# Scores of a graph attention layer summed in column groups, and x strips 6 and 7 loaded by SyncE alone

## What is computed

```
h    = relu(layernorm(x))                       # x: 8192 x 256
hp   = inlayer2 @ W.T + b ; f1 = hp @ w1 + b1 ; f2 = hp @ w2 + b2
coef = softmax(leaky_relu(f1[:,None] + f2[None,:], 0.01) masked by adj > 0)   # 8192 x 8192
out  = x + coef @ h
```

## Time and profile before

| | |
|---|---|
| time, median of 3 | 1441.95 us |
| profiled execution | 1442.37 us, its span 1440.5 us |
| granted TensorE clock, mean | 0.992 |
| TensorE matmul busy | 1409.4 us (98%) |
| VectorE busy | 1280.3 us (89%) |
| ScalarE, GpSimd busy | 612.8 us (43%), 263.6 us (18%) |
| DMA | 302.43 MB, mean 210 GB/s |

### The profile page before, as it was taken

The page is one execution under the profiler, slowest core; times in us unless marked ns, Lnnn a source line. Parts: engine busy times, 40 slices in busy tenths (PEclk is TensorE's granted clock), DMA queues, the critical chain, the costliest instruction groups (busy, mean ns, idle before and its releaser), DMA issues.

```text
span 1440.5 us, 33339 instructions
## 1 busy us (share of the span) xinstructions
PE 1409.4 (98%) x12623; PEld 1245.9 (86%) x12623; DVE 1280.3 (89%) x1315; ACT 612.8 (43%) x713; POOL 263.6 (18%) x266
## 2 busy tenths in 40 slices
PE   8589999999999999999999999999999999999998
PEld 7378888888888888888888888888888888888887
DVE  5999999899898998989889898998989989899894
ACT  2895434444343443434444344443434434344330
POOL 0682111111110110111111011111101101111110
PEclk9799999999999999999999999999999999999999
DMA  9979999999999999999999999999999999999940
GB/s 292 321 174 210 231 232 231 232 233 216 209 210 207 218 209 209 215 206 213 211 212 210 207 216 209 210 216 208 210 207 217 210 208 216 207 212 213 210 106 13
DMA packets 110184, 302.43 MB, mean 210 GB/s; under 512 B 11732, under 2 KB 44628, under 8 KB 110164
## 3 DMA queue, kind: packets, MB, share of 16 engines
q1 hardware_dynamic: 100080, 289.52, 89.8%
q10 hardware_dynamic: 10084, 12.65, 3.0%
HBM read 293.73 MB, written 8.39 MB: 210 GB/s over the span
## 4 chain that ended last, share of the span: by engine, by line
PE 93%; DMA 2%; ACT 2%; SPq 1%; DVE 1%; issue 0%; ACTq 0%; DVEq 0%
PE acc L1048 61%; PE acc L1050 31%; DMA adj_sb<-in_adj_dram 1%; SPq L336 1%; DMA adj_sb<-in_L_gnn_inlayer_dram 1%; ACT h_f L582 1%; PE rp L1003 0%; ACT rp L566 0%; DVE wgt L837 0%; DVE wT L847 0%; PE rp L1011 0%; ACT mask L566 0%; DVE wT L731 0%; ACT H L588 0%; ACTq L336 0%
## 5 line engine op out<-in xcount | busy, mean ns | idle before, releaser
L1048 PE MATMUL acc<-H,wT 128*128 128x257 f16 x8192 | 1356.8, 274 | 8.0 <-DVE wT L847 4.5
L1050 PE MATMUL acc<-H,wT 128*128 128x257 f16 x4096 | 1120.3, 274 | 0.0
L1048 PEld LDWEIGHTS acc<-H,wT 128*128 128x128 bf16 x8192 | 802.3, 98 | 111.5 <-DVE wT L847 5.7
L566 ACT ACTIVATE mask<-adj_sb 128x1024 bf16<-128x1024 int32 x504 | 519.6, 1053 | 539.2 <-DVE wgt L837 430.9
L847 DVE STREAM_TRANSPOSE wT<-wgt 128x1024 f32<-128x1024 f32 x512 | 633.6, 1238 | 128.5 <-PE acc L1050 128.4
L837 DVE SCALAR_TENSOR_TENSOR wgt<-b_word,c_word,mask 128x1024 f32<-128x1024 f32 x504 | 627.8, 1258 | 0.0
L1050 PEld LDWEIGHTS acc<-H,wT 128*128 128x128 f16 x4096 | 401.5, 98 | 50.6
L486 POOL TENSOR_TENSOR x_res<-o_room,x_res 128x256 f32<-128x256 f32 x63 | 64.6, 1026 | 1099.6 <-ACT o_room L573 1072.7
L573 ACT ACTIVATE o_room<-acc,r_den 128x256 f32<-128x256 f32 x63 | 29.8, 473 | 234.4 <-DVE r_den L866 234.4
L491 POOL TENSOR_TENSOR o_room<-o_room,x_res 128x256 f32<-128x256 f32 x63 | 81.2, 1289 | 5.3
L488 POOL TENSOR_SCALAR o_room<-h_mean,no_nb 128x256 f32<-128x256 f32 x63 | 60.0, 953 | 0.0
(11 more groups left out here) (93 smaller groups left out, 163.7 us busy)
## 6 DMA issues: line engine op xcount, KB each, us to landing
adj_sb<-in_adj_dram SPq DMA_DIRECT2D x504, 512.0 KB, 8.6
x_res<-in_x_dram SPq DMA_DIRECT2D x64, 128.0 KB, 4.0
out_dram<-o_room SPq DMA_DIRECT2D x63, 128.0 KB, 4.3
H<-in_x_dram ACTq DMA_DIRECT2D x16, 256.0 KB, 12.9
H<-in_x_dram SPq DMA_DIRECT2D x16, 256.0 KB, 13.1
adj_sb<-in_adj_dram ACTq DMA_DIRECT2D x8, 512.0 KB, 14.8
wgt<-in_L_gnn_inlayer_dram ACTq DMA_DIRECT2D x8, 256.0 KB, 9.8
wgt<-in_L_gnn_inlayer_dram SPq DMA_DIRECT2D x8, 256.0 KB, 10.2
```

Source lines behind the costliest of these rows:

```text
L566: nc.scalar.activation(place, adj_sb[:, c, g * CQ:(g + 1) * CQ], ACT.Relu, scale=M_SCALE).then_inc(m_ready, 1)
L1048: pe.matmul(acc[:, par, 0:DV], w_hi[:, slot, t, :], H[:, j, part, 0:DV], start=(j == 0 and part == 0), stop=False)
L1050: mm = pe.matmul(acc[:, par, 0:DV], w_lo[:, slot, t, :], H[:, j, 0, 0:DV], start=False, stop=(j == ROWS - 1))
```

## The change

1. `f_of_strip` uses a `V` with a quarter of the columns and writes its 8 matmuls to four column groups of 32 output partitions; a new `f_sums` adds the four groups on TensorE, so `chunk_f` becomes `chunk_turn` (transpose) and, after `f_sums`, `chunk_max`. Chunk 0 is treated between `turn_in2(5)` and `turn_in2(7)`. After each strip but the last four 128x128 matmuls on `ones` are added (`keep_busy`).
2. ScalarE: `f_to_sbuf(1)` stands before `sums(1)`; `squares(1)` goes from before `D_big` to after c; VectorE's `raw_stats` 20 to 32 go behind `low` and in among the `pack`s.
3. x strips 6 and 7 come from the sync engine alone (it had half of each); of row 0's chunk 1 the scalar engine issues three quadrants, the sync engine one.
4. The masks of rows 0 and 1 get an order of their own (`mask_order`): row 0's (2,1) and (3,1) go ahead of row 1's (0,0) and (2,0). Row 1's second chunk is issued after (0,3,1), ahead of (1,2,0).
5. VectorE does `raw_stats(60, 64)` and `variance(7)` ahead of `weights(0,1,1)` and `low_of_values(7)` after it. GpSimd's `rstds(2)` and `rstds(7)` move.

```diff
@@ sync engine
-            load_x(sp, 4, 8, (0, 1))
-            first_adj(sp, 1, (0, 1))
+            load_x(sp, 4, 6, (0, 1))
+            load_x(sp, 6, 8, (0, 2, 1, 3))
+            first_adj(sp, 1, (0,))
@@ mask order, used by whoever waits for a mask
+        mask_order = ((0, 0, 0), (0, 1, 0), (0, 2, 0), (0, 3, 0), (0, 0, 1), (0, 1, 1), (0, 2, 1),
+                    (1, 0, 0), (1, 1, 0), (0, 3, 1), (1, 2, 0), (1, 3, 0), (1, 0, 1), (1, 1, 1),
+                    (1, 2, 1), (1, 3, 1))
@@ GpSimd
             rstds(0)
-            rstds(2)
             scale_D()
             affine(0)
+            rstds(2)
             rstds(1)
...
             D_column(4)
+            rstds(7)
+            affine(7)
             low_of_values(10)
-            rstds(7)
             D_column(5)
-            affine(7)
@@ ScalarE
             load_x(act, 4, 5, (2, 3))
-            sums(1)
             f_to_sbuf(1)
             load_x(act, 5, 6, (2, 3))
-            squares(1)
-            load_x(act, 6, 7, (2, 3))
+            sums(1)
             act.wait_ge(f2_rel_ready, 1)
...
-            load_x(act, 7, 8, (2, 3))
-            values(0)
             act.wait_ge(t_ps_ready, 1)
             nc.scalar.activation(c_f32...)
+            squares(1)
+            values(0)
             high_of_values(0)
             mask_part(0, 0, 0)
             mask_part(0, 1, 0)
-            first_adj(act, 1, (2, 3))
+            first_adj(act, 1, (2, 1, 3))
...
             mask_part(0, 1, 1)
+            mask_part(0, 2, 1)
             mask_part(1, 0, 0)
             mask_part(1, 1, 0)
+            mask_part(0, 3, 1)
+            second_adj(act, 1, (2, 3))
             mask_part(1, 2, 0)
             mask_part(1, 3, 0)
-            mask_part(0, 2, 1)
-            mask_part(0, 3, 1)
-            second_adj(act, 1, (2, 3))
@@ VectorE
-            for k in range(2, NS):
-                turn_in2(k)
-            chunk_f(0)
+            ... turn_in2(5)
+            chunk_turn(0)
+            turn_in2(6)
+            chunk_max(0)
+            turn_in2(7)
+            chunk_turn(1)
+            chunk_max(1)
             raw_stats(16, 20)
-            chunk_f(1)
-            raw_stats(20, 24)
...
+            raw_stats(24, 28)
             then_wait(pack_b(0))
+            raw_stats(28, 32)
             then_wait(pack_b(1))
+            variance(3)
...
             weights(0, 0, 1)
+            raw_stats(60, 64)
+            variance(7)
+            weights(0, 1, 1)
             low_of_values(7)
-            weights(0, 1, 1)
             weights(1, 0, 0)
@@ TensorE
+            def keep_busy(n):
+                for _ in range(n):
+                    pe.matmul(acc[:, 0, 0:P], ones[:, :], ones[:, :], start=True, stop=True)
             def f_of_strip(k):
                 pe.wait_ge(in2T_ready, 2 * (k + 1))
-                for m in range(FM):
-                    mm = pe.matmul(rp[:, k // SC, ...], V[:, m, :], in2T[:, k % 2, m, :], ...)
+                for e in range(2):
+                    for g in range(Q):
+                        m = 2 * g + e
+                        mm = pe.matmul(rp[B * g:B * (g + 1), k // SC, ...], V[:, m, :],
+                                       in2T[:, k % 2, m, :], start=(e == 0), stop=(e == 1))
+            def f_sums(c):
+                pe.wait_ge(f_cols_ready, c + 1)
+                for a in range(Q):
+                    mm = pe.matmul(f_sum_ps[B * a:B * (a + 1), c * ROWS:(c + 1) * ROWS], same[:, :],
+                                   parts[:, a, :, :, 0], start=True, stop=True)
+                mm.then_inc(f_sum_ps_ready, 1)
...
+            f_of_strip(7)
             pe.wait_ge(f2_of_ready, 1)
             b_exponents(0)
+            f_sums(1)
```

More of the change, by code:

```diff
@@ L139, in graph_attention @@
         F_ps = small[:, 1, 384:385]
+        f_sum_ps = small[:, 0, 256:256 + 2 * ROWS]
         hs_ps = small[:, 1, 0:D]
@@ L210, in graph_attention @@
         f_rows_ready = sem("f_rows_ready")
+        f_cols_ready = sem("f_cols_ready")
+        f_sum_ps_ready = sem("f_sum_ps_ready")
         f2_of_ready = sem("f2_of_ready")
@@ L291, in nth_part, with nth_mask @@
             return two_rows.index((I, g, c)) + 1 if first_two(I) else 8 * I + (Q * c + g + 1)
+        def nth_mask(I, g, c):
+            return mask_order.index((I, g, c)) + 1 if first_two(I) else 8 * I + (Q * c + g + 1)
         def nth_strip(I, k):
@@ L361, in second_adj @@
         def second_adj(eng, c, quadrants):
-            eng.wait_ge(m_ready, nth_part(0, Q - 1, c))
+            eng.wait_ge(m_ready, nth_mask(0, Q - 1, c))
             load_adj(eng, 1, c, quadrants)
@@ L667, in _ @@
             values(9)
+            high_of_values(9)
             values(10)
-            high_of_values(9)
             high_of_values(10)
@@ L755, in _, with chunk_turn, chunk_max @@
             dve.wait_ge(pick_ready, Q + 1)
[L756 to L761, removed]
+            nc.vector.tensor_copy(f2_of[:, :].rearrange("p (q s) -> p q s", q=Q),
+                                  same[:, :].rearrange("p (q v) -> p q v", q=Q)[:, :, Q].unsqueeze(2)
+                                  .broadcast_to([P, Q, B])).then_inc(f2_of_ready, 1)
+            def chunk_turn(c):
                 dve.wait_ge(f_rows_ready, c + 1)
                 dve.wait_ge(in2T_ready, 2 * SC)
-                then_wait(nc.vector.transpose(f_cols[:, c * CQ:(c + 1) * CQ], f_rows[:, c * CQ:(c + 1) * CQ]))
-                then_wait(nc.vector.tensor_copy(f_col[:, at, :], f_cols[:, c * CQ:(c + 1) * CQ].rearrange(
-                    "p (j o v) -> p j o v", o=2, v=B // 2)[:, :, :, 0]))
+                nc.vector.transpose(f_cols[:, c * CQ:(c + 1) * CQ], f_rows[:, c * CQ:(c + 1) * CQ]).then_inc(f_cols_ready, 1)
+            def chunk_max(c):
+                at = slice(c * ROWS // NCH, (c + 1) * ROWS // NCH)
+                dve.wait_ge(f_sum_ps_ready, c + 1)
+                then_wait(nc.vector.tensor_copy(f_col[:, at, :], f_sum_ps[:, c * ROWS:(c + 1) * ROWS].rearrange(
+                    "p (j o) -> p j o", o=2)))
                 then_wait(nc.vector.reduce_max(tiny[:, 6 + c:7 + c], f_col[:, at, 1], AX.X))
@@ L787, in variance @@
                                         ALU.add).then_inc(var_ready, 1)
-            for k in range(2, NS):
-                turn_in2(k)
-            chunk_f(0)
+            turn_in2(2)
+            turn_in2(3)
+            turn_in2(4)
+            turn_in2(5)
+            chunk_turn(0)
[4 more added lines that the diff above has]
+            chunk_max(1)
             raw_stats(16, 20)
-            chunk_f(1)
-            raw_stats(20, 24)
             dve.wait_ge(u_ready, Q + 1)
@@ L798, in _ @@
             nc.vector.reduce_max(tiny[0:1, 1:2], fm_ps, AX.X).then_inc(f_max_ready, 1)
-            variance(2)
-            raw_stats(24, 28)
             dve.wait_ge(F_ps_ready, 1)
@@ L809, in _ @@
             nc.vector.tensor_scalar(low[:, :], t_row[:, :], -1.0, 0.0, ALU.mult, ALU.min).then_inc(low_ready, 1)
-            variance(3)
+            raw_stats(20, 24)
+            variance(2)
             def low_of_values(n):
@@ L830, in weights @@
             def weights(I, g, c):
-                dve.wait_ge(m_ready, nth_part(I, g, c))
+                dve.wait_ge(m_ready, nth_mask(I, g, c))
                 if first_two(I) and c == 1 and g == 0:
@@ L905, in _ @@
             turn(1, 2)
-            raw_stats(60, 64)
             low_of_values(9)
             turn(0, 4)
-            variance(7)
             turn(1, 3)
@@ L921, in _ @@
             turn(0, 7)
+            low_of_values(15)
             turn(1, 6)
-            low_of_values(15)
             weights(2, 0, 0)
@@ L1018, in _ @@
             pe.wait_ge(u_ready, Q)
-            for k in range(NS):
-                f_of_strip(k)
+            f_of_strip(0)
+            keep_busy(4)
+            f_of_strip(1)
+            keep_busy(4)
+            f_of_strip(2)
+            keep_busy(4)
+            f_of_strip(3)
+            keep_busy(4)
+            f_of_strip(4)
+            keep_busy(4)
+            f_of_strip(5)
+            keep_busy(4)
+            f_sums(0)
+            f_of_strip(6)
+            keep_busy(4)
+            f_of_strip(7)
             pe.wait_ge(f2_of_ready, 1)
             b_exponents(0)
+            f_sums(1)
             pe.wait_ge(ident_ready, 1)
```

15 lines of the change are left out of this document (7 added, 8 removed).

## The result

The changed kernel takes 1449.26 us (median of 5, 1448.32 to 1452.15) against 1441.98 us for the kernel before on the same chip (5 runs, 1441.65 to 1442.88). The ratio is 1.0052, interval [1.0041, 1.0062]: slower by 7.3 us, where 4.9 were forecast. The profiled execution took 1448.32 us, its span 1446.4 us (before 1440.5: +5.9), its mean granted clock was 0.987.

What follows compares the result with a forecast made beforehand. Time was taken as the moment TensorE goes into unbroken work plus a constant: `turn(1,0)` +6.1 us, less the 1.20 us wait behind it, gives +4.9, 1446.8 us on the median; range 1439.8 to 1450.5.

Steps and rivals of the forecast that it cites:

- The forecast case: Load queues: x strips 6 and 7 starve beside adjacency, `turn(1,0)` slips; net +4.9 us, range 1444.7 to 1450, chance 0.50.
- the 3 us of the scores are eaten by the 4.1 us of squares that now stand behind them: ScalarE ahead of the first mask: the scores' lead is lost; -0.1 or +1.2 us at `weights(0,0,0)`, +0.5 taken.
- the two cases for `b_exponents(1)`: TensorE from 44.9 us: 1.88 us at full clock or 3.14 at half, so c ready at 48.7 or 50.0.
- `keep_busy` costs nothing: TensorE between the score strips: the added matmuls take no time, as TensorE waits for loads there.
- say moving at 57.0: Scalar queue: adjacency of row 0's chunk 1 starts moving at 57.0 us, leaving q1 alone from 55.4 for 0.4 MB.
- strip 6 is there at 66 us: Sign of being wrong: x strip 6 landed by 66 us, where 71.5 was forecast (bounds 67.5 and 73.5).
- `turn(1,0)` at 94.5: VectorE ahead of row 1's first product: `turn(1,0)` ends at 94.5 us, +6.1 us against before.
- -1.2: TensorE ahead of row 1's second chunk: the 1.20 us wait vanishes, as VectorE has 3.8 us less behind `turn(1,0)`.
- rival 2: Faster: the scores' lead gets through and TensorE restarts without its half-clock stretch; -3.0 us, 1438.9 us, chance 0.12.
- 1: Rival on the queues: they share so that x and adjacency keep their times; +0.2 us, 1442.2, chance 0.25.
- 3: Rival on the scores: fp32 in column groups doesn't overlap, on top of the starved queue; +8 us, 1450, chance 0.06.
- 4: Rival on the scores: f isn't sooner, without the queues' effect; +2.5 us, 1444.4, chance 0.07.

Runs made afterwards that it cites:

- the kernel with the issues in between: Whole change, queues divided as before (edit 3 undone), scalar engine's half of x strip 6 issued behind c, of strip 7 behind `squares(1)`: 1440.84 us.
- the kernel without `keep_busy`: Whole change, edit 3 undone, scalar engine's halves of strips 6 and 7 issued behind `squares(1)`, added matmuls removed: 1446.13 us.
- The two kernels with the late issues: Whole change, edit 3 undone, scalar engine's halves of strips 6 and 7 issued behind `squares(1)`: 1442.01 us; the same without edits 4 and 5: 1445.72 us.

## Why the prediction came out as it did

**Which case.** The forecast case happened. Strips 6 and 7 crawl beside the scalar queue's adjacency, VectorE stands for strip 6 ahead of `turn(0,0)`, and the 1.20 us behind `turn(1,0)` vanish. The measured +7.3 us lies inside its own range (1444.7 to 1450) and near its late end; the profiled +5.9 is nearer to the +4.9.

**Scores.** Right: 1.07 us a strip (1.1 forecast), VectorE's transpose at 40.34 (40.4). The step "the 3 us of the scores are eaten by the 4.1 us of squares that now stand behind them" held in the main: `D_big` starts 3.3 us earlier than before (45.28 against 48.54), and behind `squares(1)` the first mask is only 0.6 us early, at 55.01. The remainder had the wrong sign: `weights(0,0,0)` at 56.12 is 0.8 us early where +0.5 was taken. Of the two cases for `b_exponents(1)` the full clock came, and c was ready at 47.73 (48.7). In this stretch the granted clock was (length; busy of PE, PEld, DVE, ACT, POOL; PEclk, DMA share, GB/s):

```profile
44.00:46.00 2.00, 1.61 (x5) 0.97 (x6) 1.39 (x9) 1.20 (x6) 0.36 (x1) 1.00 1.04 308
46.00:48.00 2.00, 1.52 (x10) 1.05 (x8) 1.97 (x5) 1.97 (x4) 1.37 (x5) 1.00 1.03 328
```

against 0.50 in rows 10. The sum holds only because no x issue stands in ScalarE's way any more: with those issues left where edits 1 and 2 put them the first mask is 3.5 us late, a term that the prediction didn't have. Also "`keep_busy` costs nothing" was only half of what there was to say: it gains, by some 1.9 us in the kernel with the issues in between. None of this reached the time here, since the lead ended in the wait for strip 6.

**Queues: right rates, and strip 6 with luck.** The rates were right: 0.18 and 0.046 MB/us for 0.17 and 0.05, 0.24 for q1 alone against 0.25. The start of the scalar queue's adjacency, "say moving at 57.0", was not: it was issued at 54.23, and the queue carried nothing of note until 59.2. By the prediction's own sum that should have brought strip 6 sooner: q1 moved 0.93 MB from 55.4 to 59.2, not 0.4, so 0.09 + 1.05 - 0.93 = 0.21 MB were left, 4.6 us at 0.046: about 63.8 us, and "strip 6 is there at 66 us" was my sign of being wrong. It landed at 73.0 (71.5, bounds 67.5 to 73.5) because the sum divides bytes by a mean rate, and the last parts were far behind the mean: 58 of the 64 counts were in at 63.5. The two errors, too short a time alone for q1 and no lag of the last parts, cancelled to 1.5 us. Beside the large pieces the lag is longer than beside equal ones, where the last count came at 64.3; why some parts lag at all is open. The five quadrants ended near 74, not 72, and the rest lies later than forecast: strip 7 at 79.1 (76, past its bound of 78), chunk 1 at 81.8 (79, where the terms add to 78.3; bounds to 81), row 1's chunk at 86.5 (85).

The Trainium skill has a rule that fits better than the one that I weighed: DMA: Bandwidth & Descriptors, "Queues, rings and completion order", has each DMA engine take turns between its queues packet by packet. The trace agrees in its counts, 627 packets beside 624. What I drew from the same page of the Trainium skill, "Issuing engines are not separate DMA queues", that the issuing engine matters little, doesn't hold for this kernel's time: moving half of two strips to the one queue and a quadrant to the other cost 7.8 us.

**`turn(1,0)`.** "`turn(1,0)` at 94.5" was 97.5, +9.1 where +6.1 was forecast: 1.5 us of it from strip 6, and from there 24.4 us where I counted 23.0. The difference is 0.24 us for strip 7, 0.70 for the moved `variance(7)`, which I had left out ahead of `turn(1,0)` though I counted it as gone behind it, and 0.71 for the mask behind the two DMA issues (0.3 forecast). That the slow low at 78.38 would not repeat was right (1.21 at 89.40).

**Behind it.** "-1.2" was -2.9: from row 1's first product to its second chunk 17.3 us (114.86 - 97.53) in place of 20.3. The wait is 0.34 us and not 1.20; the rest is the start at half clock, which went too, and which I had priced at 1.6 us and given to rival 2 alone. TensorE had been at work from 90.86 until its 1.34 us wait, and its steps at 97.53 are at full clock. So the sum's two errors, +3.0 and -1.7, partly cancel and leave +6.2 at row 1's second chunk where +4.9 was forecast, and the profiled execution at 1448.32 against 1447.3. The medians are 1.3 us further apart than the profiled executions: that of the changed kernel is the lowest of its five, and that of the kernel before (1442.37) lay 0.4 above its median.

**Rivals.** 1 is refuted by edit 3 alone (+7.8). 2 had the right parts: with the issues in between, its gains show (x in time, c early, no wait of 1.2 us), and where it had 1438.9 that kernel took 1440.84. It needed another edit than the one that was made. 3 and 4 fell with the 1.07 us strip and the transpose at 40.34.

## What to carry to other kernels

Where two queues shared the DMA engines here, they shared by packets: x in 1 KB pieces beside adjacency in 4 KB pieces got a fifth of the bytes. And a strip has landed when its last part is in, here 9 us after the mean rate would have it. Before moving a load to the other queue, list for both what each carries at each moment and in which pieces, and keep the transfer that is needed next away from a neighbour with larger ones. A queue must be fed before it runs dry, here some 5 us before while the other one was busy, but not while it is full, since the issue then holds the engine's own work; the best place was between two blocks of work where both were true. And an edit's gain is to be read against the next wait in line: the new orders are worth about 1.4 us and `keep_busy` about 1.9 in the kernel with the issues in between, and neither shows in the time while a load is late.

## What the hardware showed that I had not expected

- From issue to data took about 5 us on a queue that had run empty beside a busy one: issued at 54.23, moving at 59.2; issued at 53.25, moving at 58.6 in the kernel without `keep_busy`. Where both queues had been empty it took 2: in the changed kernel the issue of 91.67 moved data from 93.9, in the kernel before the one of 86.63 from 88.8. Why the busy queue costs 3 us more is open. In the meantime one queue alone moved 0.24 MB/us (0.19 in the kernel without `keep_busy`), where two together move 0.347.
- An issue of one x strip quarter took 0.4 us where the queue had room and up to 3.15 us where it was full.
- With adjacency in 1 KB pieces on one queue and x in 1 KB pieces on the other the sum is only 0.243 MB/us, against 0.347 with x on both. A packet's time is 71 ns (16 engines x 5 us x 1.136, their summed share, / 1283 packets) against 49 (80 x 1.104 / 1796). Why is open; x on q1 alone took 69 ns too (48 x 1.091 / 761).
- The two kernels with the late issues and the one with the issues in between have two groups of times 3 to 5 us apart. In the kernel without `keep_busy` the profile of a long execution shows a dry queue and late landings behind it; for the others no profile caught a long execution, and the cause is open.
